# Transposes of the fifth to eighth token tile taken in one go, and eight projections in tile order

## The chip, the cores and the metric

The kernel runs on one core of one Trainium2 chip. The metric is the device time of one execution in microseconds (us). The kernel before takes 472.58 us (median of 3 runs, 472.14 to 472.69).

## The reference, cut to what matters

The input is x, 2048 tokens of 512 values in float32. Everything starts from the layer norm of x:

```
xn  = (x - mean) / sqrt(var + 1e-5)
q, k, v = xn @ Wq + bq, xn @ Wk + bk, xn @ Wv + bv        # 32 query heads, 8 key/value heads, D = 16
s   = softmax(q k^T / 4 over the 16 x 16 matrix of each token) v
nx  = xn * rsqrt(mean(xn^2) + 1e-5) * ln_w
f   = (silu(nx @ gate^T) * (nx @ up^T)) @ down^T           # hidden size 1792
out = x + s * silu(f)
```

The attention works inside each token (16 by 16 scores, summed over heads), so the query heads are added four by four before the projection, and q, k and v of a token are 3 x 128 columns. The large part is the gated feed-forward with its three products.

## The kernel before

Tokens come in tiles of 128. Eight tiles make a pair of blocks (tiles 0 to 3 and 4 to 7), and there are two such pairs. Every float32 product on TensorE is made of three products in the chip's fp32r type: each operand is split into a high part (written by ScalarE's copy into fp32r) and a low part (operand minus high part, a subtraction on VectorE or GpSimd), and high x high, high x low and low x high are added up in PSUM. The feed-forward's gate and up products of a pair of blocks are made by a Strassen scheme of seven products (M1 to M7) on sums of blocks; the sums of z are made by `t_add`, their high parts by `t_hi` on ScalarE and their low parts by `t_lo` on VectorE. A group g is one of the 14 slices of 128 hidden columns; group 0 of the first pair is the exception and is computed plainly (`first_products`, `gate1(0)`, `up1(0)`), while the rest is being prepared. The seven products start with `m1(1)`.

There is no planner: each engine has its instructions written out in order, and semaphores tie the engines together. The change lies in the start of the program, in this chain for tiles 4 to 7 (j is the tile, `J` is 4, `JJ` is 8):

- VectorE: `stats_tile`, `aggregate`, `variance`, `mean_of` (lines 1100 to 1123) give mean and variance of a tile. `x_variance` (line 1127) gives another variance of four tiles for the later scale of the projection.
- GpSimd: `rms_of(0, J, ...)` (lines 494, 495 and 497, two powers and a product) waits for `x_variance(0)`. Behind it stand `scale_tile(J)` and `scale_tile(J + 1)` (lines 487 and 490, a power and a product), the sum of the biases (541, 544), two more `scale_tile`, a second `rms_of`, and the low part of the down weights (512).
- ScalarE: `z_tile` (868) normalises x in place, and waits for the shift of its tile.
- TensorE: `second_tile` (763) transposes the four 128 x 128 pieces of a tile (line 760) into a bank of PSUM. It waits for `z_tile`, and for `z_raw` of the tile four earlier, which used the bank before.
- ScalarE: `z_hi_tile` (880) copies the bank into the high part, VectorE: `z_lo_tile` (1167) subtracts it from the bank, ScalarE: `z_raw_tile` (884) copies the bank to SBUF; it waits for the low part.
- VectorE: `t_add(0, 0)` (1190) waits for all eight `z_raw`.

Beside it run the projections. `qkv_product(index)` is 12 matmuls of 384 columns: eight with the high weights (744, 745), then four with the low weights (749). Its first call waits for both low halves of the weights, which `lo_qkv` (1341) writes on VectorE. `qkv_take(index)` (1244) reads the result out on VectorE and counts `qkv_out` up. Projection 0 uses bank 3, projection 1 bank 0, projection 2 bank 1, and then bank 3 and bank 0 take turns (3 in bank 0, 4 in bank 3, 5 in bank 0, 6 in bank 3, 7 in bank 0). So `qkv_product(index)` waits for `qkv_out` of index - 1. `m1(1)` takes bank 3, and waits for `qkv_out` of 7, that is for `qkv_take(6)`. `QKV_ORDER` holds which tile a projection is of.

The order of VectorE behind this stands in lines 1370 to 1394: takes, `t_add`, the weights of group 1 (`lo_a(1)`, `sums(1)`, `lo_s(1)`), `times_up0(0)`, `times_up1(0)` and `t_lo`. In group 1, ScalarE's order is `seed(1)`, `t_hi(0, 3)` (waits for `t_add(0, 3)`), `hi_a(2)`, `hi_wd(1)`, `take_u2(1)` (931), and TensorE's `m7(1)` waits for `take_u2(1)`.

Of the kernel before, what the change touches and what calls it, by code (L numbers as in the profile page):

```python
# [52 lines left out]
def build(nc, x, wq, bq, wk, bk, wv, bv, lnw, gate_up, down, out):  # L53
# [3 lines left out]
    J = TB // P  # L57
# [4 lines left out]
    JJ = 2 * J  # L62
    WARM_UP = 32
    SLOTS = 13
    QKV_ORDER = ((0, 1, 2, 4, 5, 6, 7, 3), (0, 1, 2, 3, 4, 5, 6, 7))
    GATE_BANK, UP_BANK = 1, 2
    LAST = GROUPS - 1

# [9 lines left out]
    with ExitStack() as ctx:  # L78
# [6 lines left out]
        def sem(name):  # L85
            return ctx.enter_context(nc.semaphore(name))
# [56 lines left out]
        def qkv_bank(index):  # L143

            if index == 2:
                return GATE_BANK
            return 3 * (1 - index % 2 if index < JJ else index % 2)
# [19 lines left out]
        d_done, qkv_done, transposed = sem("d_done"), sem("qkv_done"), sem("transposed")  # L167
# [21 lines left out]
        def wait(eng, s, value):  # L189
            if value > 0:  # L190
                eng.wait_ge(s, value)
# [47 lines left out]
            return w_late[:, u - LATE] if u >= LATE else wd_ops[:, u % 3]  # L239

        def qkv_index(tile):
            return JJ * (tile // JJ) + QKV_ORDER[tile // JJ].index(tile % JJ)

        def parts(f, j):

# [315 lines left out]
        def _(pe):  # L561
# [159 lines left out]
                    down_tile(u, j)  # L721

            def qkv_product(index):
                pair = index // JJ
                j = QKV_ORDER[pair][index % JJ]
                if pair:
                    pe.wait_ge(z2_lo_done, 2 * (j // J) + 2)
                else:
                    pe.wait_ge(z_lo_done, j + 1)
                if index in (JJ, JJ + 1):  # L730

                    pe.wait_ge(h0_done, NI - 1 + index - JJ)
                if index == 2:
                    pe.wait_ge(silu0_done, 1)
                else:
                    wait(pe, qkv_out, index - 1)
                acc = gu_ps[:, qkv_bank(index), 0:QKV]
                zi, t = 2 * (j // J), slice((j % J) * P, (j % J + 1) * P)
                z_h = [z_hi[:, zi + k // 2, k % 2, t] for k in range(K)]
                z_l = [z_lo[:, zi + k // 2, k % 2, t] for k in range(K)]  # L740
                for k in range(K):
                    if index == 0:
                        pe.wait_ge(wqkv_hi_done, k // 2 + 1)
                    pe.matmul(acc, z_h[k], wqkv_hi[:, k, :], start=k == 0, stop=False)  # L744
                    pe.matmul(acc, z_l[k], wqkv_hi[:, k, :], start=False, stop=False)  # L745
                for k in range(K):
                    if index == 0:
                        pe.wait_ge(wqkv_lo_done, k // 2 + 1)
                    end = pe.matmul(acc, z_h[k], wqkv_lo[:, k, :], start=False, stop=k == K - 1)  # L749
                end.then_inc(qkv_done, 1)  # L750
# [12 lines left out]
            def second_tile(j):  # L763
                pe.wait_ge(z_raw_done, j - J + 1)
                transpose_tile(y_ps[:, j - J, :], j)
# [6 lines left out]
            first_products()  # L772
            qkv_product(0)
            qkv_product(1)
            second_tile(J)
            second_tile(J + 1)
            qkv_product(2)
            second_tile(J + 2)
            second_tile(J + 3)
            qkv_product(3)  # L780
            qkv_product(4)
            gate1(0)
# [42 lines left out]
        def _(act):  # L825
# [33 lines left out]
            def hi_wd(n):  # L859
                act.wait_ge(wd_in[n % 2], 16 * (n // 2 + 1))  # L860
                wait(act, d_done, J * (n - 2))
                wait(act, wd_stored[n % 3], 16 * (n // 3))
                act.activation(wd_ops[:, n % 3, 0, :], wd_raw[:, n % 2, :], ACT.Copy).then_inc(wd_hi_done, 1)  # L863

            def z_tile(j):
                t = slice(j, j + 1)
                act.wait_ge(z_shift_done, j - J + 1)
                act.activation(xz[:, j, :], xz[:, j, :], ACT.Identity, bias=z_shift[:, j - J:j - J + 1],
                               scale=z_scale[:, t]).then_inc(z_act_done, 1)
# [6 lines left out]
            def z_hi_tile(j):  # L876
                act.wait_ge(transposed, j + 1)
                zi, t = 2 * (j // J), slice((j % J) * P, (j % J + 1) * P)
                dst = z_hi[:, zi:zi + 2, :, t].rearrange("p m c t -> p (m c) t")
                act.activation(dst, y_ps[:, j % J, :].rearrange("p (k t) -> p k t", k=K), ACT.Copy).then_inc(z_hi_done, 1)  # L880
# [23 lines left out]
            def t_hi(pair, n):  # L904
                zi, k, b = ((ZT1, 0, 0), (ZT3, 0, 1), (ZT2, 2, 1), (ZT4, 2, 0))[n]
                act.wait_ge(t_added, 4 * pair + n + 1)
                if zi == ZT4:

                    act.wait_ge(qkv_done, JJ * (pair + 1) - (pair == 0))
                    act.wait_ge(m3_done, NI if pair else 1)  # L910
                act.activation(z_hi[:, zi, :, :], zT[pair][:, k:k + 2, b * TB:(b + 1) * TB], ACT.Copy).then_inc(t_hi_done, 1)

# [94 lines left out]
            z_tile(J)  # L1007
            z_tile(J + 1)
            hi_wd(0)
            z_hi_tile(J)  # L1010
            z_tile(J + 2)
            z_hi_tile(J + 1)
            z_tile(J + 3)
            z_raw_tile(J)
            z_hi_tile(J + 2)
            z_raw_tile(J + 1)
# [80 lines left out]
        def _(dve):  # L1097
# [27 lines left out]
            def x_variance(first):  # L1125
                t = slice(first, first + J)
                dve.tensor_scalar(x_var[:, t], mean_var[:, t, 1], EPS, None, ALU.add).then_inc(var_done, 1)
# [35 lines left out]
            def z_lo_tile(j):  # L1163
                bank = y_ps[:, j % J, :]
                zi, t = 2 * (j // J), slice((j % J) * P, (j % J + 1) * P)
                dve.wait_ge(z_hi_done, j + 1)
                dve.tensor_tensor(z_lo[:, zi:zi + 2, :, t].rearrange("p m c t -> p (m c) t"),
                                  bank.rearrange("p (k t) -> p k t", k=K),
                                  z_hi[:, zi:zi + 2, :, t].rearrange("p m c t -> p (m c) t").bitcast(F32),
                                  ALU.subtract).then_inc(z_lo_done, 1)  # L1170
# [39 lines left out]
            def first_lo(part, places=slice(0, K)):  # L1210
                if (part, places.stop) == (0, 1):
                    dve.wait_ge(gate_hi_one, 1)
                else:
                    dve.wait_ge(w_hi_a, part + 1)
                for m, c, k in first_places(part)[places]:
                    t = slice(c * P, (c + 1) * P)
                    end = dve.scalar_tensor_tensor(w_ops[:, 0, 1, m, t], gu_raw[:, 0, 2 * m + c, :], lnw_sb[:, k:k + 1],
                                                   w_ops[:, 0, 0, m, t].bitcast(F32), ALU.mult, ALU.subtract)
                if places.stop == K:
                    end.then_inc(w_lo_a, 1)  # L1220
# [13 lines left out]
                                  ALU.subtract).then_inc(w_lo_s, 1)  # L1234

            def qkv_take(index):
                tile = JJ * (index // JJ) + QKV_ORDER[index // JJ][index % JJ]
                bank = qkv_bank(index)
                assert tile < SLOTS or taken[0] >= values_end(tile - SLOTS)
                dve.wait_ge(qkv_done, index + 1)  # L1240
                if index == 0:
                    dve.wait_ge(bias_summed, 2)
                dve.wait_ge(rms_done, (1 if index < 3 else 2) if index < JJ else 3)
                dve.scalar_tensor_tensor(qkv[:, tile % SLOTS, :], gu_ps[:, bank, 0:QKV], rms[:, tile:tile + 1], bias[:],
                                         ALU.mult, ALU.add).then_inc(qkv_out, 1)
# [92 lines left out]
            def lo_qkv(half_of_k):  # L1338
                k = slice(2 * half_of_k, 2 * half_of_k + 2)
                dve.wait_ge(wqkv_hi_done, half_of_k + 1)  # L1340
                dve.tensor_tensor(wqkv_lo[:, k, :], wqkv_raw[:, k, :], wqkv_hi[:, k, :].bitcast(F32),
                                  ALU.subtract).then_inc(wqkv_lo_done, 1)
# [12 lines left out]
            normalise_tile(2)  # L1355
            normalise_tile(3)
            first_lo(0, slice(1, K))
            x_variance(0)
            for j in range(J):
                z_lo_tile(j)  # L1360
            first_lo(1)
            for j in range(J, JJ):
                stats_tile(j)
                aggregate(j)
                variance(j)
                mean_of(j)
                if j == J:
                    lo_qkv(0)
                    lo_qkv(1)
            x_variance(J)  # L1370
            qkv_take(0)
            z_lo_tile(J)
            qkv_take(1)
            z_lo_tile(J + 1)
            times_up0(0)
            qkv_take(2)
            z_lo_tile(J + 2)
            z_lo_tile(J + 3)
            qkv_take(3)
            t_add(0, 0)  # L1380
            t_add(0, 1)
# [118 lines left out]
```

## Time and profile before

| what | us |
|---|---|
| median of 3 runs | 472.58 |
| the profiled execution | 472.32 |
| its span in the trace | 470.5 |
| TensorE busy | 465.0 |
| VectorE busy | 412.7 |
| ScalarE busy | 244.8 |
| GpSimd busy | 122.4 |

The span is the time from the first to the last event of the trace; the rest of the profiled time lies outside it. Times below are microseconds from the start of the span. TensorE has two rows: PE for the matmul itself, whose end is modelled, and PEld for the load of its weights, which overlaps the matmul before. Because matmuls are pipelined, the distance from one start to the next says more than the duration. The granted clock of TensorE is full in all 40 slices of the span.

### The profile page before, as it was taken

The page shows a single profiled execution, that of the slowest core. Times are in us where ns is not written, and L with a number is a line of the kernel's source. Part 1 is how long each engine was busy: PE and PEld are TensorE (multiplying, and loading weights), DVE is VectorE, ACT ScalarE, POOL GpSimd, SP SyncE. Part 2 cuts the span into 40 slices and gives each one's busy share as a digit, 9 for nine tenths or more (in the row PEclk, how much of TensorE's full clock was granted, in tenths as well). Part 3 has the DMA queues.
Part 4 walks back from the last instruction along what each step waited for, and adds up shares of the span by engine and source line. Part 5 has one row for each costly group of instructions (what it writes and reads, how often), then busy time and mean ns, then how long its engine had stood idle before and what let it go on. Part 6 is the DMA issues. An engine that isn't in the chain of part 4 may idle for free.

```text
span 470.5 us, 6241 instructions
## 1 busy us (share of the span) xinstructions
PE 465.0 (99%) x2134; PEld 392.0 (83%) x2134; DVE 412.7 (88%) x559; ACT 244.8 (52%) x418; POOL 122.4 (26%) x105
## 2 busy tenths in 40 slices
PE   8999999999999999999999999999999999999997
PEld 7998888888888888888888888888888888888886
DVE  6999688987898898999979898999999888888994
ACT  5794665658688888654122545325235235358002
POOL 3931213216222112144352111110001111127920
PEclk9999999999999999999999999999999999999999
DMA  8707987669689975564374759555556655513762
GB/s 261 265 4 273 348 358 269 260 256 283 145 272 308 380 303 242 173 246 155 118 259 145 237 188 355 196 195 219 214 202 224 224 201 202 201 46 134 282 255 89
DMA packets 44623, 105.70 MB, mean 225 GB/s; under 512 B 20272, under 2 KB 21808, under 8 KB 41264
## 3 DMA queue, kind: packets, MB, share of 16 engines
q1 hardware_dynamic: 44592, 105.31, 62.9%
q8 instruction: 17, 0.28, 0.2%
q14 instruction: 14, 0.11, 0.1%
HBM read 69.90 MB, written 35.40 MB: 224 GB/s over the span
## 4 chain that ended last, share of the span: by engine, by line
PE 97%; DMA 1%; DVE 1%; POOL 0%; SPq 0%; issue 0%; ACT 0%; DVEq 0%; POOLq 0%
PE gu_ps L571 18%; PE gu_ps L568 18%; PE gu_ps L570 18%; PE y_ps L715 8%; PE y_ps L714 8%; PE y_ps L713 8%; PE gu_ps L715 3%; PE gu_ps L714 3%; PE gu_ps L713 3%; PE gu_ps L745 2%; PE gu_ps L744 2%; PE gu_ps L749 2%; DMA xz<-x 1%; PE y_ps L760 1%; PE gu_ps L588 0%; PE gu_ps L589 0%
## 5 line engine op out<-in xcount | busy, mean ns | idle before, releaser
L571 PE MATMUL gu_ps<-z_hi,w_ops 128*128 128x512 f32 x378 | 147.1, 389 | 0.0
L570 PE MATMUL gu_ps<-z_lo,w_ops 128*128 128x512 f32 x378 | 147.1, 389 | 0.0
L568 PE MATMUL gu_ps<-z_hi,w_ops 128*128 128x512 f32 x378 | 147.1, 389 | 0.0
L506 POOL TENSOR_TENSOR h_lo<-h,h_hi 128x512 fp32r<-128x512 f32 x28 | 37.1, 1324 | 228.5 <-ACT h_hi L956 228.4
L568 PEld LDWEIGHTS gu_ps<-z_hi,w_ops 128*128 128x128 f32 x378 | 71.0, 188 | 14.8
L571 PEld LDWEIGHTS gu_ps<-z_hi,w_ops 128*128 128x128 f32 x378 | 70.9, 188 | 14.7
L570 PEld LDWEIGHTS gu_ps<-z_lo,w_ops 128*128 128x128 f32 x378 | 70.9, 188 | 14.7
L715 PE MATMUL y_ps<-wd_ops,h_lo 128*128 128x512 f32 x168 | 65.5, 390 | 0.0
L714 PE MATMUL y_ps<-wd_ops,h_hi 128*128 128x512 f32 x168 | 65.5, 390 | 0.0
L713 PE MATMUL y_ps<-wd_ops,h_hi 128*128 128x512 f32 x168 | 65.4, 390 | 0.0
L956 ACT ACTIVATE h_hi<-h 128x512 fp32r<-128x512 f32 x28 | 17.7, 631 | 58.9 <-DVE h L1260 58.9
L1302 DVE TENSOR_TENSOR prod<-scores,qkv 128x1024 f32<-128x1024 f32 x32 | 43.3, 1352 | 0.8
L1284 DVE TENSOR_TENSOR prod<-qkv 128x1024 f32<-128x1024 f32 x32 | 41.8, 1306 | 0.6
L1305 DVE TENSOR_REDUCE attn<-prod 128x64 f32<-128x1024 f32 x32 | 38.9, 1217 | 0.8
L1287 DVE TENSOR_REDUCE scores<-prod 128x128 f32<-128x1024 f32 x32 | 38.9, 1215 | 0.6
L713 PEld LDWEIGHTS y_ps<-wd_ops,h_hi 128*128 128x128 f32 x168 | 31.5, 188 | 6.6 <-POOL h_lo L506 0.3
L715 PEld LDWEIGHTS y_ps<-wd_ops,h_lo 128*128 128x128 f32 x168 | 31.5, 188 | 6.6
L714 PEld LDWEIGHTS y_ps<-wd_ops,h_hi 128*128 128x128 f32 x168 | 31.5, 188 | 6.4
L931 ACT ACTIVATE u<-gu_ps 128x512 f32<-128x512 f32 x27 | 16.1, 598 | 39.8 <-PE gu_ps L571 39.8
L1272 DVE TENSOR_TENSOR h_kept<-u 128x512 f32<-128x512 f32 x27 | 22.4, 830 | 12.8 <-ACT u L944 10.0
L512 POOL TENSOR_TENSOR wd_ops<-raw,wd_ops 128x512 fp32r<-128x512 f32 x14 | 19.2, 1368 | 54.9 <-ACT wd_ops L863 25.1
L506 POOL TENSOR_TENSOR h_lo<-h_kept,h_hi 128x512 fp32r<-128x512 f32 x15 | 24.4, 1628 | 34.2 <-ACT h_hi L956 33.1
(146 smaller groups left out, 753.1 us busy)
## 6 DMA issues: line engine op xcount, KB each, us to landing
w_kept<-w_ops SPq DMA_DIRECT2D x13, 1792.0 KB, 7.6
w_ops<-w_kept SPq DMA_DIRECT2D x13, 1792.0 KB, 7.3
wd_ops<-wd_kept SPq DMA_DIRECT2D x35, 512.0 KB, 3.8
raw<-gate_up SPq DMA_DIRECT2D x30, 256.0 KB, 3.9
wd_kept<-wd_ops SPq DMA_DIRECT2D x14, 512.0 KB, 8.0
xz<-x SPq DMA_DIRECT2D x16, 256.0 KB, 5.6
raw<-down SPq DMA_DIRECT2D x14, 256.0 KB, 3.9
w_ops<-wd_kept SPq DMA_DIRECT2D x7, 512.0 KB, 7.1
```

Source lines behind the costliest of these rows:

```text
L506: pool.tensor_tensor(lo, src, hi.bitcast(F32), ALU.subtract).then_inc(h_lo_done, 1)
L568: pe.matmul(acc, w_h, z_hi[:, zi, c, :], start=start and c == 0, stop=False, skip_group_check=True)
L570: pe.matmul(acc, w_h, z_lo[:, zi, c, :], start=False, stop=False, skip_group_check=True)
L571: end = pe.matmul(acc, w_l, z_hi[:, zi, c, :], start=False, stop=c == 1, skip_group_check=True)
L713: pe.matmul(acc, hi, wd[:, 0, t], start=n == 0, stop=False, skip_group_check=part)
L714: pe.matmul(acc, hi, wd[:, 1, t], start=False, stop=False, skip_group_check=part)
L715: pe.matmul(acc, lo, wd[:, 0, t], start=False, stop=n == NI - 1, skip_group_check=part)\
L1272: dve.tensor_tensor(h_kept[:, g % NI, :], u2[:], up, ALU.mult).then_inc(h1_done, 1)
L1284: return dve.tensor_tensor(pr, q[:, d:d + HALF, :].unsqueeze(2).to_broadcast([P, HALF, D, HKV]), k.unsqueeze(1).to_broadcast([P, HALF, D, ...
L1287: return dve.tensor_reduce(s[:, d:d + HALF, :], pr, X, ALU.add)
L1302: return dve.tensor_tensor(pr, e[:, d:d + HALF, :].unsqueeze(2).to_broadcast([P, HALF, HKV, D]), v.unsqueeze(1).to_broadcast([P, HALF, HKV ...
L1305: return dve.tensor_reduce(o[:, d:d + HALF, :], pr, X, ALU.add)
```

## The change

Three things are reordered; no instruction is added or taken away.

1. TensorE: the transposes of tiles 4 to 7 stand in one go behind the third projection, instead of two behind the second and two behind the third. The projections 3 to 7 are of tiles 3, 4, 5, 6, 7 instead of 4, 5, 6, 7, 3. ScalarE normalises tiles 6 and 7 ahead of the high part of tile 4, and `t_hi(0, 3)`, which overwrites the high part of tiles 4 to 7, waits for the eighth projection instead of the seventh.
2. VectorE: the low parts of tiles 4 to 7 stand behind the third take, and the low parts of the projection weights ahead of the fifth tile's statistics.
3. VectorE: `x_variance(0)` stands behind `first_lo(1)` instead of ahead of the low parts of tiles 0 to 3.

```diff
-    QKV_ORDER = ((0, 1, 2, 4, 5, 6, 7, 3), (0, 1, 2, 3, 4, 5, 6, 7))
...
         def qkv_index(tile):
-            return JJ * (tile // JJ) + QKV_ORDER[tile // JJ].index(tile % JJ)
+            return tile
...
             def qkv_product(index):
-                pair = index // JJ
-                j = QKV_ORDER[pair][index % JJ]
+                pair, j = divmod(index, JJ)
...
             first_products()
             qkv_product(0)
             qkv_product(1)
-            second_tile(J)
-            second_tile(J + 1)
             qkv_product(2)
-            second_tile(J + 2)
-            second_tile(J + 3)
+            for j in range(J, JJ):
+                second_tile(j)
             qkv_product(3)
             qkv_product(4)
             gate1(0)
...
-                    act.wait_ge(qkv_done, JJ * (pair + 1) - (pair == 0))
+                    act.wait_ge(qkv_done, JJ * (pair + 1))
...
             z_tile(J)
             z_tile(J + 1)
             hi_wd(0)
+            z_tile(J + 2)
+            z_tile(J + 3)
             z_hi_tile(J)
-            z_tile(J + 2)
             z_hi_tile(J + 1)
-            z_tile(J + 3)
             z_raw_tile(J)
             z_hi_tile(J + 2)
             z_raw_tile(J + 1)
...
             def qkv_take(index):
-                tile = JJ * (index // JJ) + QKV_ORDER[index // JJ][index % JJ]
+                tile = index
...
             first_lo(0, slice(1, K))
-            x_variance(0)
             for j in range(J):
                 z_lo_tile(j)
             first_lo(1)
+            x_variance(0)
+            lo_qkv(0)
+            lo_qkv(1)
             for j in range(J, JJ):
                 stats_tile(j)
                 aggregate(j)
                 variance(j)
                 mean_of(j)
-                if j == J:
-                    lo_qkv(0)
-                    lo_qkv(1)
             x_variance(J)
             qkv_take(0)
-            z_lo_tile(J)
             qkv_take(1)
-            z_lo_tile(J + 1)
             times_up0(0)
             qkv_take(2)
-            z_lo_tile(J + 2)
-            z_lo_tile(J + 3)
+            for j in range(J, JJ):
+                z_lo_tile(j)
             qkv_take(3)
             t_add(0, 0)
```

## Rows read from the trace of the kernel before

**Rows 1.** The page's first part: busy us, share of the span, instructions.

```profile
PE 465.0 (99%) x2134; PEld 392.0 (83%) x2134; DVE 412.7 (88%) x559; ACT 244.8 (52%) x418; POOL 122.4 (26%) x105
```

**Rows 2.** Waits of PE over the span: us in total, times, longest.

```profile
PE y_ps L760 <- DVE xz L1118: 0.5, 1, 0.5
```

**Rows 3.** Timeline of PE, 17 to 26 us: start, duration, line, xcount.

```profile
17.48 0.93 PE L749 MATMUL gu_ps<-wqkv_lo,z_hi 128*128 128x384 f32 x4
...
19.63 0.86 PE L749 MATMUL gu_ps<-wqkv_lo,z_hi 128*128 128x384 f32 x4
20.33 1.03 PE L760 MATMUL y_ps<-ident,xz 128*128 128x128 f32 x8
21.12 0.42 PE L744 MATMUL gu_ps<-wqkv_hi,z_hi 128*128 128x384 f32 x1
21.37 0.34 PE L745 MATMUL gu_ps<-wqkv_hi,z_lo 128*128 128x384 f32 x1
...
25.58 0.85 PE L749 MATMUL gu_ps<-wqkv_lo,z_hi 128*128 128x384 f32 x4
```

**Rows 4.** Timeline of DVE, 15 to 40 us.

```profile
15.91 1.82 DVE L1341 TENSOR_TENSOR wqkv_lo<-qkv,wqkv_hi 128x768 fp32r<-128x768 f32 x2
...
20.91 0.61 DVE L1244 SCALAR_TENSOR_TENSOR qkv<-gu_ps,rms,bias 128x384 f32<-128x384 f32 x1
...
25.53 0.69 DVE L1167 TENSOR_TENSOR z_lo<-y_ps,z_hi 128x512 fp32r<-128x512 f32 x1 [0.25 <-ACT z_hi L880]
26.47 0.62 DVE L1244 SCALAR_TENSOR_TENSOR qkv<-gu_ps,rms,bias 128x384 f32<-128x384 f32 x1 [0.24 <-PE gu_ps L749]
27.00 4.71 DVE L1190 TENSOR_TENSOR h_kept<-h_kept 128x1024 f32<-128x1024 f32 x3
...
34.70 0.61 DVE L1244 SCALAR_TENSOR_TENSOR qkv<-gu_ps,rms,bias 128x384 f32<-128x384 f32 x1
...
39.16 0.61 DVE L1244 SCALAR_TENSOR_TENSOR qkv<-gu_ps,rms,bias 128x384 f32<-128x384 f32 x1
```

**Rows 5.** Timeline of POOL, 14 to 30 us.

```profile
14.21 1.06 POOL L494 TENSOR_TENSOR x_rstd<-x_var,minus_half 128x4 f32<-128x4 f32 x1
15.25 1.01 POOL L495 TENSOR_TENSOR z_std<-z_var,half 128x4 f32<-128x4 f32 x1
16.34 0.58 POOL L497 TENSOR_TENSOR rms<-x_rstd,z_std 128x4 f32<-128x4 f32 x1
16.87 1.27 POOL L487 TENSOR_TENSOR z_scale<-z_var,minus_half 128x1 f32<-128x1 f32 x1
...
22.08 0.19 POOL L490 TENSOR_TENSOR z_shift<-minus_mean,z_scale 128x1 f32<-128x1 f32 x1
...
27.45 1.92 POOL L506 TENSOR_TENSOR h_lo<-h,h_hi 128x512 fp32r<-128x512 f32 x1 [1.72 <-ACT h_hi L956]
```

**Rows 6.** Timeline of ACT, 22 to 45 us.

```profile
22.74 0.80 ACT L868 ACTIVATE xz<-xz,z_shift,z_scale 128x512 f32<-128x512 f32 x1
...
24.90 0.60 ACT L880 ACTIVATE z_hi<-y_ps 128x512 fp32r<-128x512 f32 x1
25.37 0.62 ACT L884 ACTIVATE h_kept<-y_ps 128x512 f32<-128x512 f32 x1
26.26 0.60 ACT L884 ACTIVATE h_kept<-y_ps 128x512 f32<-128x512 f32 x1 [0.27 <-DVE z_lo L1167]
...
44.82 0.58 ACT L931 ACTIVATE u<-gu_ps 128x512 f32<-128x512 f32 x1
```

**Rows 7.** Timeline of PEld: the first loads of projection 6, m1(1), m7(1).

```profile
35.77 0.19 PEld L744 LDWEIGHTS gu_ps<-wqkv_hi,z_hi 128*128 128x128 f32 x1
...
39.93 0.19 PEld L568 LDWEIGHTS gu_ps<-z_hi,w_ops 128*128 128x128 f32 x1
...
45.45 0.19 PEld L568 LDWEIGHTS gu_ps<-z_hi,w_ops 128*128 128x128 f32 x1
```

**Rows 8.** Timeline of DVE, 29.0 to 29.1 us: the second t_add.

```profile
28.14 2.32 DVE L1190 TENSOR_TENSOR h_kept<-h_kept 128x1024 f32<-128x1024 f32 x1
```

## The prediction

> **What bounds the kernel now.** I read the busy shares first: TensorE is busy for 465.0 of 470.5 us [rows 1]. The waits of TensorE come next: behind its warm-up it has one wait of 0.5 us, at 9.46 us, for a normalised tile [rows 2], ahead of all that is changed. So the end is set by one unbroken stream of matmuls. Reordering can shorten it only by what a switch or a late weight costs in the stream, but any new wait of TensorE moves the end by its whole length, unless a later wait would have been there anyway. Then I read the timelines of the four engines from 10 to 48 us, asking of each wait in TensorE's order how long before its instruction it was met.
>
> **What the change can give back.** Two things. The four low-weight matmuls of projection 0 take 0.93 us, those of projection 1 take 0.86 [rows 3]: the third of them, due near 17.8, waits for the second low half of the weights, written at 15.91 + 1.82 = 17.73 [rows 4]. With both halves ahead of the fifth tile's statistics they are written near 14.85 + 1.82 = 16.7 (14.85 is 15.91 less the 1.06 of the statistics, which now come later), so 0.07 us goes. Behind a run of transposes the first matmul takes 0.25 us to the next (21.12 to 21.37) where the others take 0.17 [rows 3]; one run instead of two saves 0.08. Together TensorE could be 0.15 us earlier from projection 3 on. The transposes themselves cost (21.12 - 20.33) / 8 = 0.10 each as before.
>
> **VectorE and GpSimd up to 22 us.** VectorE's order has the same work up to `qkv_take(0)`, so this stays at 20.91 [rows 4]. Only tile 4's statistics end later, by the 1.74 us of the two weight subtractions, at 17.7. GpSimd gets `x_variance(0)` at 15.0 instead of finding it ready at 14.21 [rows 5]. Its two powers and product then run 15.0 to 18.0: the first power meets the weight subtraction that runs to 15.76. How such a meeting goes the rows show twice: the product of 16.34 took 0.58 and ended at 16.92, 0.10 behind the end of the first subtraction (16.82), and the power of 16.87 took 1.27 where later ones take 0.56, so the GpSimd operation stands until the subtraction is over. The other way round, the power of 15.25 to 16.26 was under way when the first subtraction started at 15.91, and the pair still took 1.82, twice 0.91: the long power did not hold VectorE up. So I take +0.7 for the first power, near nothing for VectorE (0.05 at most, as the first product cost it), product done at 18.0, `scale_tile(4)` 18.0 to 18.8, and `scale_tile(5)` at 18.8, which waits for tile 5's variance and is where it was. From there GpSimd is as before, with the shift of tile 7 at 22.08 + 0.19 = 22.27. The bounds are from 0 up to all of the power waiting for both subtractions, 0.9 late everywhere.
>
> A rule of the Trainium skill speaks against this reading. "SBUF — State Buffer", section "SBUF: two separate sides", says that VectorE operations with two SBUF inputs and GpSimd operations take a shared pair of ports as an exclusive lock held for the whole instruction. By it the power of 15.25 should have kept the first subtraction off until 16.26; the row shows that it didn't. For the 512-element subtraction on GpSimd the rule and the trace agree: see `h_lo` below. What it would make of the powers here is the second rival.
>
> **The exchange of tiles 4 to 7.** Before, two tiles were transposed at 20.33 and two at 23.29, and ScalarE and VectorE worked on the first two meanwhile. Now nothing can be copied before the run of 16 transposes. Projection 2 ends at 22.35 (20.33 - 0.07 + 2.09), tile 4 is out near 22.95. ScalarE has `z_tile(7)` first: shift at 22.27, start at 22.31, 0.81 long; its next instruction starts some 0.1 ahead of the end (24.90 + 0.60 and the next at 25.37 [rows 6]). So z_hi(4) starts at 23.03. TensorE needs tile 7 normalised (23.12) at 22.35 + 12 x 0.10 = 23.5: no wait. From here on the chain is worked out with z_hi and z_raw 0.60 long and 0.48 apart, z_lo 0.69 long and 0.61 apart, 0.03 to 0.04 us from one engine to the other (z_hi of 24.90 ends at 25.50, z_lo starts 25.53, ends 26.22, z_raw starts 26.26 [rows 4, 6]):
> - z_hi(4) 23.03 to 23.62; z_lo(4) 23.65 to 24.34 (the third take, possible from 22.55, is over at 23.17); z_hi(5) 23.51.
> - z_raw(4) waits for z_lo(4): 24.38; z_hi(6) 24.86 to 25.46; z_lo(6) 25.49 to 26.18; z_raw(5) 25.36; z_hi(7) 25.84 to 26.44; z_lo(7) 26.47 to 27.16; z_raw(6) 26.32.
> - z_raw(7) waits for z_lo(7): 27.20 to 27.80. `t_add(0, 0)`, which waits for it, starts at 27.83. `qkv_take(3)` fits between (27.08 to 27.70; its projection ends at 26.3).
>
> Before, `t_add(0, 0)` started at 27.00, straight behind `qkv_take(3)` [rows 4]. VectorE is 0.83 late, 0.88 with the 0.05 of the port; I take 0.85. The gate product at 28.2 needs z_lo(7) of 27.16 and is not held.
>
> **What waits for VectorE.** From 27.00 to the seventh take VectorE works without a gap, so the 0.85 stays whole: 12.2 us of back-to-back work, and ScalarE's copies that it needs (`hi_a(1)`, `t_hi`, `hi_s(1)`) keep a margin or are themselves behind VectorE. What TensorE needs of it:
> - Projection 6 loads at 35.77 [rows 7] and waits for the fifth take, which ended at 34.70 + 0.61 = 35.31 [rows 4]. Now 36.16, load at 36.20 where TensorE is ready at 35.62: a wait of 0.58, which leaves it 0.43 later than before.
> - `m1(1)` loads at 39.93 [rows 7] and waits for the seventh take: 39.16 + 0.61 = 39.77 [rows 4]. Margin 0.11 after the 0.05 of the handover. Now 40.62, load at 40.67: 0.74 later than before, a further wait of 0.31.
> - `m7(1)` loads at 45.45 [rows 7] just behind `take_u2(1)`, 44.82 + 0.58 = 45.40 [rows 6]: no margin. ScalarE's order puts this behind `t_hi(0, 3)`, which waits for `t_add(0, 3)`, the next of VectorE's late work. So it is 0.85 late, and TensorE with it: a last wait of 0.11.
> The waits sum to 1.00, less the 0.15 given back: 0.85 later at `m7(1)`. Behind it VectorE has gaps of about a microsecond in each group, all later waits hang on work that TensorE itself releases, and the loads from HBM come no later than the rest. Nothing gives the 0.85 back, since TensorE then runs unbroken to the end.
>
> Sum against the profiled execution: 470.5 + 0.85 = 471.4 of span and 472.32 + 0.85 = 473.2 of time. The median of the runs stands 0.26 higher, at 472.58: **473.4 us**, 0.18% more. This measurement can tell about 0.2% (0.95 us) from no change, so most of what I expect sits just below what can be told.
>
> **Rivals.**
> - *The powers hold the port, or wait out both subtractions.* Then the second weight subtraction or the first power is about 0.95 late, the shift of tile 7 comes at 23.2, z_tile(7) ends at 24.1, the transposes of tile 7 wait 0.55, and the whole exchange starts 0.95 later: VectorE 1.8 late, time 472.6 + 1.8 = 474.4. For it: the power of 16.87 with its 1.27. Against it: the power of 15.25, as above. By the rule of the page "SBUF — State Buffer" this is the case that would come.
> - *Not slower: the lateness is swallowed in the subtractions of z.* `h_lo` on GpSimd asked at 27.45, got the port when the first `t_add` was over and ran to 29.37 [rows 5], and the second `t_add` took 2.32 instead of 1.22 [rows 8]: 1.1 us of VectorE's chain. If the shifted order lets `h_lo` run beside something else, VectorE is 0.85 - 1.1 = 0.25 early, no take holds TensorE, and only the 0.15 shows: 472.4. It decides as soon as VectorE's lateness at the seventh take is below 0.11. Against it: `h_hi` stands directly behind z_raw(7) in ScalarE's order as before, so `h_lo` asks 0.5 us into the first `t_add` again, and every VectorE instruction behind it to the end of the sums has two SBUF inputs.
> - *The same waits, shorter*: handovers or a rest of margin that I can't see make the lateness 0.3 to 0.6, time 473.0. This is the forecast's own spread, not a case by itself.
>
> **How the numbers follow.** Forecast 0.72, with its own range of 472.9 to 473.9 (0.3 to 1.3 late, run to run spread included); ports 0.15; not slower 0.13. Slower by over 0.2% needs 473.53: a third of the forecast (0.24) and all of the ports: 0.39. Faster by over 0.2% needs 471.6, which no term reaches; 0.05 for what I don't see. Within: 0.56. The range takes in the 0.15 gain below and the ports above: 472.3 to 474.5.
>
> **What would show it.** In the changed profile: low-weight matmuls of projection 0 in 0.86 instead of 0.93; one run of 16 transposes from 22.35; z_hi(4) near 23.0, z_raw(7) near 27.2 and the first `t_add` near 27.8; loads of projection 6 near 36.2, `m1(1)` near 40.7, `m7(1)` near 46.3, each right behind its take or copy; then all later matmuls 0.85 late. If the shift of tile 7 is past 22.5, the ports are the reason; if the second `t_add` takes 1.2, it is the second rival. I am wrong if the first `t_add` starts before 27.3 or TensorE shows a wait elsewhere.

## The result, and the profile after

| kernel | median us | lowest to highest | runs |
|---|---|---|---|
| before | 472.58 | 471.91 to 472.80 | 11 |
| changed | 473.64 | 472.96 to 474.00 | 11 |

The ratio is 1.0025 (95% interval 1.0016 to 1.0033), 1.06 us more. A second measurement (the changed kernel again, below) gave 1.0032 (1.0020 to 1.0045). The profiled execution took 473.2 us, its span is 471.4. The forecast was 473.4, and 471.4 for the span. The direction is right, the time is 0.24 us above the forecast, and the three waits that it named are there. One term behind it is wrong, and the agreement of the span to the tenth is luck, as the traces show.

The changed kernel's waits of TensorE over the whole span (engine, what waited, for what: us in total, times, longest), which answer to [rows 2]; PE first, then the weight loads (PEld). "issue" stands where the profile shows nothing that the engine waited for, so these waits are named by what ends just before them in the timelines:

```profile
PE y_ps L767 <- POOL ident L474: 1.5, 1, 1.5
PE gu_ps L742 <- DVE qkv L1240: 0.5, 1, 0.5
PE y_ps L758 <- DVE xz L1114: 0.4, 1, 0.4
```

```profile
PEld gu_ps L742 <- issue: 1.0, 2, 0.8
...
PEld y_ps L758 <- issue: 0.4, 1, 0.4
PEld gu_ps L567 <- issue: 0.3, 1, 0.3
...
PEld gu_ps L567 <- ACT u L927: 0.2, 1, 0.2
```

There is a new wait for a take (`qkv_take`, now line 1240), and behind it one at `m1(1)` and one at `m7(1)`, the three that the forecast named. L758 in the second fence is a fourth, which the forecast had ruled out: the transposes of tile 7 stood 0.35 for their normalised tile. The loads of projection 6, `m1(1)` and `m7(1)` in the timeline of PEld, which answer to [rows 7] (35.77, 39.93, 45.45 before):

```profile
36.31 0.19 PEld L742 LDWEIGHTS gu_ps<-wqkv_hi,z_hi 128*128 128x128 f32 x1 [0.79 <-issue]
...
40.77 0.19 PEld L567 LDWEIGHTS gu_ps<-z_hi,w_ops 128*128 128x128 f32 x1 [0.32 <-issue]
...
46.33 0.19 PEld L567 LDWEIGHTS gu_ps<-z_hi,w_ops 128*128 128x128 f32 x1 [0.23 <-ACT u L927]
```

Forecast: 36.20, 40.67, 46.30. The chain of work that ended last, between 20 and 37 us of the changed kernel (start, length), where before it was TensorE's matmuls alone:

```profile
20.92 0.51 POOL z_scale L486
...
21.51 0.20 POOL z_shift L489
...
21.73 1.58 ACT xz L864 x2
23.32 0.49 ACT z_hi L876
23.83 0.70 DVE z_lo L1163
24.56 0.60 ACT h_kept L880
...
26.66 0.70 DVE z_lo L1163
27.38 0.61 ACT h_kept L880
28.01 3.47 DVE h_kept L1186 x2
...
35.67 0.54 DVE qkv L1240
36.34 0.41 PE gu_ps L742
```

It starts on GpSimd with the scales of tiles 6 and 7, runs through the exchange, the three `t_add` and VectorE's order to the fifth take, and enters TensorE at projection 6. The three `t_add` take 4.72, as before (4.71 [rows 4]), so `h_lo` on GpSimd still costs the second of them its 1.1: the rival in which the lateness is swallowed there did not come. Then the start of the program, timelines of PE, DVE and POOL of the changed kernel (start, duration):

```profile
16.93 0.85 PE L747 MATMUL gu_ps<-wqkv_lo,z_hi 128*128 128x384 f32 x4
...
21.79 2.30 PE L758 MATMUL y_ps<-ident,xz 128*128 128x128 f32 x16
23.84 0.42 PE L742 MATMUL gu_ps<-wqkv_hi,z_hi 128*128 128x384 f32 x1
```

```profile
14.28 0.16 DVE L1123 TENSOR_SCALAR x_var<-mean_var 128x4 f32<-128x4 f32 x1
14.35 1.81 DVE L1337 TENSOR_TENSOR wqkv_lo<-qkv,wqkv_hi 128x768 fp32r<-128x768 f32 x2
...
21.01 1.14 DVE L1240 SCALAR_TENSOR_TENSOR qkv<-gu_ps,rms,bias 128x384 f32<-128x384 f32 x2 [0.50 <-issue]
...
28.01 4.72 DVE L1186 TENSOR_TENSOR h_kept<-h_kept 128x1024 f32<-128x1024 f32 x3
```

```profile
14.52 2.53 POOL L493 TENSOR_TENSOR x_rstd<-x_var,minus_half 128x4 f32<-128x4 f32 x1 [0.83 <-DVE x_var L1123]
17.02 1.01 POOL L494 TENSOR_TENSOR z_std<-z_var,half 128x4 f32<-128x4 f32 x1
...
22.28 0.19 POOL L489 TENSOR_TENSOR z_shift<-minus_mean,z_scale 128x1 f32<-128x1 f32 x1
```

The reader is to see two things that cancel. TensorE's low-weight matmuls of projection 0 start at 16.93, where they started at 17.48 [rows 3]: the start of the program, all that comes before projection 0 and that I call the front, was 0.55 early in this execution, since the third x tile landed earlier (its statistics start at 5.28 instead of 5.83). And GpSimd's first power took 2.53 us instead of 1.06 [rows 5], so the shift of tile 7 came at 22.28, later than the 22.08 of before in spite of the early front. The first `t_add`, forecast at 27.83, started at 28.01: 0.55 early by the front, and 0.7 late by the power. To take the front out, all traces below are read by one distance: from the first low-weight matmul of projection 0 on PE to the first `t_add` on DVE. Before it is 27.00 - 17.48 = 9.52, in the changed kernel 28.01 - 16.93 = 11.08; the forecast's 0.83 would have been 10.35. A second reading takes the front out of the end: the span less the start of the same matmuls. It is 453.0 in both traces of the kernel before (470.5 - 17.48, 470.6 - 17.57) and 454.5 in the changed kernel (471.4 - 16.93), 1.5 us more with the long power. The span is given to 0.1 us, and so is this difference. Nothing is given back behind `m7(1)`: from its load to the end of the span it is 425.05 before and 425.07 after.

### The profile page after: what moved, and what is told of

It reads as the page before. It is cut to its first block, busy times and chain, and to the rows that moved or that the text cites. A ratio compares the mean times of both kernels' runs of the same rounds, so it can differ in the third digit from the quotient of the medians.

```text
span 471.4 us, 6241 instructions
## 1 busy us (share of the span) xinstructions
PE 465.4 (99%) x2134; PEld 391.7 (83%) x2134; DVE 412.6 (88%) x559; ACT 244.7 (52%) x418; POOL 122.5 (26%) x105
## 4 chain that ended last, share of the span: by engine, by line
PE 92%; DVE 2%; ACT 1%; POOL 0%; issue 0%; DVEq 0%; POOLq 0%
PE gu_ps L567 18%; PE gu_ps L569 18%; PE gu_ps L570 18%; PE y_ps L713 8%; PE y_ps L714 8%; PE y_ps L712 8%; PE gu_ps L714 3%; PE gu_ps L713 3%; PE gu_ps L712 3%; PE gu_ps L742 2%; PE gu_ps L743 1%; PE gu_ps L747 1%; DVE h_kept L1186 1%; ACT h_kept L880 0%; ACT xz L864 0%; ACT z_hi L876 0%
```

## The experiments

Theory A was the forecast as it stood: all of the cost is in the exchange of tiles 4 to 7. Theory B: beside it GpSimd waits out both weight subtractions. The later names are B1 (it is the meeting of the power with subtractions that have two SBUF inputs) and C (waits of TensorE on one late chain don't add). Each kernel was timed together with the kernel before on the same chip.

### The changed kernel again

> The changed kernel again, for a second trace of it beside one of its start. In the first trace the whole front, from the second pair of x tiles on, ran 0.55 us earlier than in the profile of the kernel before, while the shift of the eighth tile came 0.2 us later. Theory A (the lateness of VectorE in the exchange of tiles 4 to 7 is the forecast's 0.85, whatever the front does): time 0.85 over the kernel before. Theory B (beside it GpSimd's first power stands until both weight subtractions are over, 0.75 more): with an equal front 1.6 over the kernel before, with an early one 1.0. In both, the first t_add near 28.0 with an early front; with a late one 27.85 by A and 28.5 by B. Measured so far: 1.06 over.

Measured: 473.73 us against 472.16, ratio 1.0032 (1.0020 to 1.0045). Its timeline of POOL has the long power again, with a late front (projection 0 at 18.16, the first `t_add` at 29.05, distance 10.89):

```profile
15.56 2.52 POOL L493 TENSOR_TENSOR x_rstd<-x_var,minus_half 128x4 f32<-128x4 f32 x1 [0.83 <-DVE x_var L1123]
```

The median's 1.57 more is B's 1.6 and not A's 0.85, though the first measurement had 1.06. The first `t_add` came later than either theory had said (27.85 and 28.5), for the front was later still. By the second reading this execution costs 1.3 (472.5 - 18.16 = 454.3). What was late in this front wasn't an x tile: ScalarE's first operation on the gate and up weights stood 1.29 us for their load, and VectorE 0.97 for ScalarE (ACT):

```profile
8.64 1.28 ACT L836 ACTIVATE w_ops<-raw,lnw_sb 128x128 fp32r<-128x128 f32 x4 [1.29 <-DMA raw<-gate_up]
```

### x_variance early

```diff
             first_lo(0, slice(1, K))
+            x_variance(0)
             for j in range(J):
                 z_lo_tile(j)
             first_lo(1)
-            x_variance(0)
             lo_qkv(0)
             lo_qkv(1)
```

> The changed kernel with x_variance(0) back ahead of the low parts of tiles 0 to 3; all else as changed. Theory A (GpSimd's order of waits doesn't matter for the time): the same time as the changed kernel within 0.1 us. Theory B (the first power asks for its ports while the two weight subtractions run and stands for 1.5 us; asked earlier it runs free): first power 1.05 long instead of 2.53, the shift of tile 7 about 0.75 earlier against the front, no idle time of VectorE ahead of the first take, no wait in the transposes, time 0.7 under the changed kernel and 0.3 to 0.85 over the kernel before.

Measured: 473.15 against 472.16, ratio 1.0017 (1.0008 to 1.0026), 0.58 under the changed kernel of the same chip. POOL and the first take on DVE:

```profile
14.23 1.06 POOL L493 TENSOR_TENSOR x_rstd<-x_var,minus_half 128x4 f32<-128x4 f32 x1
15.27 1.41 POOL L494 TENSOR_TENSOR z_std<-z_var,half 128x4 f32<-128x4 f32 x1
```

```profile
20.94 1.13 DVE L1240 SCALAR_TENSOR_TENSOR qkv<-gu_ps,rms,bias 128x384 f32<-128x384 f32 x2
```

The first power is free, the second stands 0.4 with the first subtraction, the take has no idle time before it. The distance is 28.01 - 17.71 = 10.30, the forecast's 0.8, and the span less the start 453.7 (471.4 - 17.71), 0.7 over the kernel before. By the medians it is 0.99 over, where B had said 0.3 to 0.85. The intervals of two ratios overlap, so it is the traces that carry the difference, and the medians only agree with it.

### VectorE's parts alone

The kernel before with the diff's last part, cut to `x_variance(0)` and `lo_qkv`:

```diff
             first_lo(1)
+            x_variance(0)
+            lo_qkv(0)
+            lo_qkv(1)
             for j in range(J, JJ):
...
-                if j == J:
-                    lo_qkv(0)
-                    lo_qkv(1)
```

> The kernel before with VectorE's parts of the change alone: x_variance(0) behind first_lo(1), both weight subtractions ahead of the fifth tile's statistics; the transposes stay two and two. Theory A: the late weight of projection 0 goes, nothing else, time 0 to 0.1 under the kernel before. Theory B: GpSimd is 0.75 late with the shifts of tiles 4 and 5, which the first two transposes at 20.3 now wait for; TensorE stands 0.5 to 0.7 there, and the time is 0.4 to 0.7 over the kernel before.

Measured: 472.99 against 472.16, ratio 1.0016 (1.0007 to 1.0025): 0.83 more, a little over B's 0.7, and A's gain isn't there. The power took 2.52. The waits of the loads show where TensorE stood:

```profile
PEld y_ps L760 <- issue: 0.8, 2, 0.5
```

These are the transposes of tiles 4 and 5. So this part costs without the other: it makes the shifts of tiles 4 and 5 late, and TensorE needs them early in this order.

### The transposes in one go alone

The changed kernel with `x_variance(0)` and `lo_qkv` as before.

> The changed kernel with VectorE's order of x_variance(0) and the weight subtractions as before: the transposes in one go, with their low parts behind the third take, alone. Theory A: all of the change's cost is here, 0.85 over the kernel before, and the same as the changed kernel within 0.1. Theory B: 0.75 less than the changed kernel, if both start with the same front; over the kernel before by the 0.83 of the exchange less the 0.08 of the one switch (the first t_add at 27.8 instead of 27.0 with a late front). A third, that the exchange costs nothing and GpSimd's wait is all: the time of the kernel before within 0.1.

Measured: 473.05 against 472.16, ratio 1.0020 (1.0012 to 1.0029): 0.89 more, where B had said 0.75, and 0.68 under the changed kernel. This is the exchange by itself, with the free power, and its trace follows the forecast to 0.1 us. ACT and DVE:

```profile
22.98 1.09 ACT L876 ACTIVATE z_hi<-y_ps 128x512 fp32r<-128x512 f32 x2
24.34 0.60 ACT L880 ACTIVATE h_kept<-y_ps 128x512 f32<-128x512 f32 x1 [0.26 <-DVE z_lo L1163]
...
27.17 0.60 ACT L880 ACTIVATE h_kept<-y_ps 128x512 f32<-128x512 f32 x1 [0.27 <-DVE z_lo L1163]
```

```profile
27.80 4.72 DVE L1186 TENSOR_TENSOR h_kept<-h_kept 128x1024 f32<-128x1024 f32 x3
```

Forecast: z_hi(4) 23.03, z_raw(4) 24.38, z_raw(7) 27.20, `t_add` 27.83. The distance is 27.80 - 17.43 = 10.37, against 9.52; the span less the start is 453.8 (471.2 - 17.43), 0.8 more.

### Statistics between the two subtractions

```diff
             lo_qkv(0)
-            lo_qkv(1)
             for j in range(J, JJ):
...
                 mean_of(j)
+                if j == J:
+                    lo_qkv(1)
```

> The changed kernel with the fifth tile's statistics between the two weight subtractions. Theory B1 (the first power on GpSimd waits for its ports until no subtraction with two SBUF inputs is running; back to back they give it no gap): the power asks 0.16 into the first subtraction, gets in when it ends and is 1.6 long instead of 2.5; the shift of the eighth tile comes about 0.75 earlier against the front, time 0.6 under the changed kernel, as with x_variance early. Rival B2 (the power is long because it starts cold behind an idle GpSimd, not because of the ports): 2.5 long as before, time as the changed kernel.

Measured: 473.22 against 472.30, ratio 1.0018 (1.0010 to 1.0027), 0.92 more. POOL:

```profile
15.31 1.65 POOL L493 TENSOR_TENSOR x_rstd<-x_var,minus_half 128x4 f32<-128x4 f32 x1 [0.83 <-DVE x_var L1123]
```

GpSimd had been idle for as long as in the changed kernel (0.83), and asked as late (0.16 us into the subtraction that started at 15.15), but here it had to wait for one only: 1.65, and a distance of 10.30. This is what B1 had said. One trace alone doesn't decide it, since the next kernels show 1.66 with the two subtractions still back to back. What excludes B2, that the power is long because it comes behind an idle GpSimd, is the kernel before with a late `x_variance(0)`, below: there the first power comes behind the same 0.83 of idle time, meets no subtraction, and takes 1.01.

### qkv_take(4) earlier, then qkv_take(6), then take_u2(1)

Three kernels, each the one before it and one step more:

```diff
             t_add(0, 2)
+            qkv_take(4)
             lo_a(1)
             sums(1)
             times_up1(0)
-            qkv_take(4)
```

```diff
-            lo_s(1)
             qkv_take(6)
+            lo_s(1)
```

```diff
+                if g == 1:
+                    take_u2(g)
                 hi_a(g + 1)
                 hi_wd(g)
-                take_u2(g)
+                if g > 1:
+                    take_u2(g)
```

> The changed kernel with qkv_take(4) ahead of lo_a(1), sums(1) and times_up1(0). Theory C (waits of TensorE on one late chain don't add: only the last one counts): the wait at projection 6 of 0.5 to 0.6 us goes, the wait at m1(1) takes it over, the time is that of the changed kernel within 0.1. Rival (each wait costs its own length): 0.5 under the changed kernel.

> As the last, and qkv_take(6) ahead of lo_s(1) as well. Theory C: projection 6 and m1(1) are not held by a take; the lateness is all paid at m5(1), for lo_s(1), and at m7(1), for take_u2(1): time of the changed kernel, at most 0.1 under it. Rival: 0.8 under the changed kernel.

> As the last, and ScalarE's take_u2(1) straight behind t_hi(0, 3), ahead of hi_a(2) and hi_wd(1). Theory C: the last wait is shortened by the two ScalarE copies, 1.25 us: m7(1) is held 0.4 at most beyond the kernel before, time 0.9 to 1.2 under the changed kernel, 0.2 to 0.5 over the kernel before. Rival (something behind m7(1) is late too, such as t_lo(0, 3) for m4(1)): at most 0.5 under the changed kernel.

Measured against 472.30: 473.72, ratio 1.0026 (1.0015 to 1.0038); 473.59, 1.0026 (1.0017 to 1.0035); 472.83, 1.0008 (0.9999 to 1.0016). TensorE's waits, one fence for each kernel:

```profile
PE gu_ps L567 <- DVE qkv L1240: 0.5, 1, 0.5
```

```profile
PE gu_ps L567 <- ACT u L927: 0.5, 1, 0.5
```

```profile
38.69 0.19 PEld L742 LDWEIGHTS gu_ps<-wqkv_hi,z_hi 128*128 128x128 f32 x1 [0.36 <-issue]
```

(The third is the timeline of PEld: the load of projection 7, 0.36 us idle before it.) The first step took the wait at projection 6 away, and `m1(1)` stood 0.5 instead. The second took that away, and `m7(1)` stood 0.5. Neither changed the time: 1.42 and 1.29 over the kernel before, within the 1.06 and 1.57 of the changed kernel, which wasn't timed beside these three. The third took away the last wait of the chain, and with it 0.76 us; I had expected 0.9 to 1.2. What is left is projection 7, which stands for `qkv_take(5)` (37.96 to 38.57 on VectorE), with a power of 2.52 in this trace. The span less the start has to be compared at one length of the power. With the short one it is 453.8 and 453.8 (471.0 - 17.18, 471.3 - 17.51), about as in the two kernels above with a free power (453.7 and 453.8). With the long one it is 454.3 to 454.5 in the changed kernel and 453.5 (471.3 - 17.84) with all three steps, 0.8 to 1.0 less. So waits on one late chain don't add up: as long as one is left that was met late, it collects.

One more thing stands in these traces. The order of the first 17 us is that of the changed kernel, yet the power took 1.66 in the first two and 2.52 in the third. With the other three of that order (2.53, 2.52, 2.52) it is four times the long one and twice the short one, always asking 0.16 to 0.17 into the subtraction. POOL of the kernel with `qkv_take(4)` early:

```profile
14.77 1.66 POOL L493 TENSOR_TENSOR x_rstd<-x_var,minus_half 128x4 f32<-128x4 f32 x1 [0.83 <-DVE x_var L1123]
```

Its distance is 27.57 - 17.18 = 10.39, that of the long ones 10.89 to 11.08 with the transposes in one go. Part of that spread is TensorE's own start. From VectorE's first weight subtraction to the first `t_add` it is 13.65 or 13.66 in all three with the long power (28.01 - 14.35, 29.05 - 15.40, 28.73 - 15.07) and 12.97 or 12.96 in both with the short one (27.57 - 14.60, 27.92 - 14.96): the second subtraction costs the chain 0.69.

### The kernel before again

> The kernel before again, for a second trace of it: where the landing of x puts the front in another execution. If the front (the third tile's statistics) and the first t_add move together, and GpSimd's first power is 1.05 long in both traces, the spread between executions of one kernel is the landing of x; the changed kernel has a second source of spread, the power that took 2.52 in some traces and 1.66 in others. Span 470.2 to 470.9.

Measured in one execution: 472.42 us, span 470.6, power 1.07, distance 27.04 - 17.57 = 9.47. The third tile's statistics started 0.22 earlier than in the first trace, and TensorE's stream 0.09 later, since the first tile was the late one here: the spread of the landing is real, but this pair is too close to show how far it carries.

### The weights early, x_variance as before; and the reverse

The kernel before with `lo_qkv(0)` and `lo_qkv(1)` ahead of the fifth tile's statistics, and the kernel before with `x_variance(0)` behind `first_lo(1)`.

> The kernel before with the two weight subtractions ahead of the fifth tile's statistics and x_variance(0) where it was. It differs from the kernel with both of VectorE's parts (0.83 over the kernel before) only in x_variance(0). Theory B1: the first power asks ahead of the subtractions and is 1.05 long, the second one may stand 0.4; the shift of tile 4 is where it was within 0.1, and the first two transposes wait for nothing: the time of the kernel before within 0.15, and the low-weight matmuls of projection 0 take 0.86. Rival B3 (the early subtractions do the harm by the later statistics of tile 4): 0.5 to 0.8 over the kernel before.

> The kernel before with x_variance(0) behind first_lo(1) alone; the weight subtractions stay behind the fifth tile's statistics. Theory B1 (it is the meeting with back-to-back subtractions that costs, not the later request): the first power asks during the statistics, which have one input, and is 1.05 long; the second asks 0.2 into the first subtraction and stands 0.4 to 1.5 with it. The shift of tile 4 comes 0.4 to 1.2 later than in the kernel before, and the transposes due at 20.33 are held by what of it exceeds the margin of 1.0 that this tile has: time 0 to 0.5 over the kernel before, under that of the kernel with both of VectorE's parts (0.83 over). Rival (the later request alone makes the 0.83): 0.7 to 0.9 over.

Measured: 472.48 against 472.45, ratio 1.0002 (0.9993 to 1.0011), low-weight matmuls of projection 0 in 0.85; and 472.49 against 472.55, ratio 0.9999 (0.9990 to 1.0008). Either move alone costs nothing that can be measured, both together cost 0.83: it is the meeting. The rivals B3 (the later statistics of tile 4) and the later request by itself, which asked for 0.5 to 0.9, fall. In the first kernel the first power took 1.07 and the second 1.41, as forecast. In the second kernel the first power asks during the statistics and the second one into the subtraction, and it got in between the two; the shift of tile 4 came 0.5 later (18.69 against 18.22), inside the margin of its transposes (POOL):

```profile
15.11 1.01 POOL L494 TENSOR_TENSOR x_rstd<-x_var,minus_half 128x4 f32<-128x4 f32 x1 [0.83 <-DVE x_var L1127]
16.09 1.73 POOL L495 TENSOR_TENSOR z_std<-z_var,half 128x4 f32<-128x4 f32 x1
```

### All of it cured

The changed kernel with `x_variance(0)` early, both takes early and `take_u2(1)` early: the diffs above together.

> The changed kernel with x_variance(0) early, qkv_take(4) ahead of lo_a(1), qkv_take(6) ahead of lo_s(1), and take_u2(1) straight behind t_hi(0, 3). Theory C with B1: both latenesses are cured or out of TensorE's way, and what is left is the 0.15 that the forecast let TensorE gain (one switch less, no late weight): 0.15 under the kernel before to 0.1 over it, 1.3 under the changed kernel. Rival (the change costs TensorE something else, such as the wait for the transposes of tile 8): 0.3 or more over the kernel before.

Measured: 472.13 against 472.45, ratio 0.9997 (0.9988 to 1.0005). TensorE is held by no take, `take_u2` or tile any more; its waits from projection 0 on are 0.2 us of loads, and the 0.3 for `h_lo` that the kernel before has too. The first `t_add` is as late as with the transposes in one go (27.95 - 17.63 = 10.32), and nothing waits for it. So the lateness is still there and costs nothing. The 0.15 us that the forecast gives TensorE would be 472.30 here; the measurement can't tell it from nothing. No version that I ran is shown to be faster than the kernel before.

## Why the prediction was right, and which term was not

- *TensorE is an unbroken stream, so only a new wait counts.* Right: 465.4 us busy after, and three waits in its order make the difference. Windows of 60 us from 60 to 420 have TensorE busy for all of their length in both kernels: nothing was given back later.
- *0.15 given back.* The 0.07 is seen (0.93 to 0.85; in the second trace of the kernel before it was 0.87 already). Of the 0.08 for one switch less only 0.03 is: the gap behind the run is spared, but the 16 transposes take 1.66 in one go where twice eight took 2 x 0.79. From the low-weight matmuls of projection 0 to the start of `gate1(0)` it is 10.87 in the kernel before, 10.80 with the weights early, and 10.77 with the weights early and the transposes in one go: 0.10 in all. That is below what can be measured, in line with the cured kernel.
- *The exchange makes VectorE 0.83 late.* Right, to 0.02 in the distance (10.37 - 9.52 = 0.85) and in each step, in the kernel with the transposes in one go alone.
- *TensorE pays at projection 6, m1(1) and m7(1), and the last wait decides.* Right: loads in that kernel at 36.10, 40.55 and 46.12; and moving the first two waits away didn't change the time. But the forecast also said that the transposes of tile 7 wait for nothing, and that a wait of TensorE elsewhere would prove it wrong. They waited in each trace with the long power and the transposes in one go, 0.35, 0.22 and 0.23 (PEld), and in none with the short or the free one.
- *GpSimd's first power: I take +0.7.* This is the mis-sized term. It was 0.6 (1.66 long) in two traces of six and 1.5 (2.52 long) in four. I had argued from the product that slipped in between the subtractions before (0.58 long, [rows 5]) that there is a gap. There is, but not in each execution: in four of the six the power missed it and stood 1.5 instead of 0.7.
- *`scale_tile(5)` is where it was, so the shift of tile 7 stays.* This holds with the short power only. With the long one the shift came 0.75 later against the front (22.28 - 16.93 = 5.35 against 22.08 - 17.48 = 4.60), and the distance was 0.5 to 0.7 longer than the exchange alone makes it. The forecast's own mark for this, the shift of tile 7 past 22.5, wasn't passed as the clock reads (22.28 to 22.47), but it was with the 0.55 of the early front taken out. The rival on the ports had the mechanism "waits out both subtractions" and priced it 0.95 late where 0.69 was measured; I had given it a chance of 0.15. Its other half, that the power holds VectorE up, didn't happen: the pair of subtractions took 1.81 or 1.82 in every trace with a waiting power.
- *473.4.* The exchange and the three waits, which make most of the time lost, were right for the reasons given. That the number agrees so closely is partly luck. The profiled execution agreed to the tenth (span 471.4) because its early front, 0.55, hid most of the long power. By the span less the start, the two executions of the changed kernel, both with the long power, cost 1.5 and 1.3, and those with a short or free power and the transposes in one go 0.7 to 0.8, where the forecast had 0.85 for all and the rival 1.8. The medians of 473.64 and 473.73, 1.06 and 1.57 over the kernel before, fit a mixture of long and short powers; how many of the executions without a trace had the long power isn't known. I had split "slower" from "same" at 0.2%: the ratio of 1.0025 is past that and its interval (1.0016 to 1.0033) is not, and the two kernels with a free power lie at 1.0017 and 1.0020, so the runs don't settle on which side of that line the change is.

## What to carry to other kernels

Where one engine's stream is unbroken, list for each wait in it by how much it was met early: moving work on another engine costs that work's lateness less the smallest of these margins that comes behind it, and the waits of one chain don't add up. So find all waits that the late chain reaches before curing any: here curing the first, and then the first two, only moved the bill, and the gain came with the third. The last one alone was never tried; by the forecast's own sum it would give back 0.11, since `m1(1)` already stands for 0.74 of the 0.85. And before an event that starts small GpSimd operations is moved, look at what VectorE does at the new moment: back-to-back subtractions with two SBUF inputs can shut GpSimd out for as long as they run.

## What the runs showed of the hardware

- A GpSimd power of 128 x 4 that asked 0.16 us into the first of two back-to-back VectorE subtractions (128 x 768, 0.94 to 0.95 each, 1.81 the pair) got its turn either between them (1.66 long) or behind both (2.52 to 2.53), in four of six executions behind both. Alone it takes 1.02. A power that asked at another moment, 0.08 into the first (16.09 against 16.01, 1.73 long) or 0.4 into it (1.41 long in three traces), got in between each time. What decides between the two at 0.16 I didn't find in the traces.
- Once let in, it ran for some 0.88 more (to 14.52 + 2.53 = 17.05 in the changed kernel, where the pair of subtractions ended at 14.35 + 1.81 = 16.16), nearly its full length: it stands at its start. A power that had started wasn't stopped, and it didn't stop VectorE: [rows 4, 5], the power of 15.25 to 16.26 (1.01 long) and the pair of subtractions from 15.91 on (1.82 long).
- The Trainium skill ("SBUF — State Buffer", section "SBUF: two separate sides") tells of an exclusive lock for the whole instruction, where a VectorE operation has two SBUF inputs and a GpSimd operation reads SBUF. The trace agrees as far as the GpSimd operation's wait goes, and for `h_lo` (128 x 512), which kept the second `t_add` for 1.1 us [rows 8]; for the powers it doesn't hold from GpSimd's side.
- The landing of the first loads moves the front by up to 1.2 us between executions of the same kernel (projection 0's low weights at 16.93 and at 18.16), about as much as the change itself costs, so a single trace must not be read without it. The early one had its third x tile 0.55 earlier than the kernel before; the late one stood for its first gate and up weights.
